# Row maxima of a two-pass attention softmax: high terms only, four heads at once in row strips, read from the transposed q and k

## The chip, the cores and the metric

The kernel runs on one core of a Trainium2 chip. The metric is the device time of one execution in microseconds (us). The engines are PE (TensorE, matmuls), DVE (VectorE), ACT (ScalarE), POOL (GpSimd) and SP (SyncE, which issues all DMAs here). Each has its own program, and semaphores order them.

## The reference, cut to what matters

Sixteen sequences of 256 tokens and 512 features pass through an adaptive RMS norm, 16-head self attention (32 features per head), an output projection with a skip, and a feed-forward with ternary weights and a GELU.

```python
q = _rms_norm(q, g_q); k = _rms_norm(k, g_k)
logits = jnp.einsum('bhqd,bhkd->bhqk', q, k) * d ** (-0.5)
attn = jax.nn.softmax(logits, axis=-1)
o = jnp.einsum('bhqk,bhkd->bhqd', attn, v)
o = o + o @ W_out
h = bitlinear(layer_norm(o), w_fc)       # 512 -> 2048, ternary weights
h = gelu(h)
x = x + bitlinear(layer_norm(h), w_proj) # 2048 -> 512, ternary weights
```

## The kernel before

Sequences are pipelined. One iteration works on five of them in different stages: `late` (end of the second feed-forward layer), `ffn` (output projection, first layer), `att` (attention), `qkv` (projections, transposes) and `pre` (statistics of the input). Iterations -2 to 17 run; the stages att and ffn are both present in 1 to 15. Iteration 0 has att without ffn and turns the feed-forward weights into ternary ones. Iteration 15 has no qkv stage, 16 no att.

Precision comes from splitting numbers into a high and a low half in f16. After the q and k projections, PE transposes four pieces into `T`, ACT writes the high part and DVE the low part of `qkT` (128 partitions = four heads of 32 features, by 4 groups, by LO_Q, HI_Q, HI_K, LO_K, by 256 tokens). SP then copies it with 16 DMAs into `stk`: for each of the 16 heads 96 rows that hold high and low parts stacked, so that one matmul with K=96 gives the full product. A 97th row holds minus the row maximum on one side and ones on the other.

Attention first computes for each head the logits with the queries on the partitions (L642, K=96, two matmuls of 256 columns, one for each half of the queries) in bank SA or SB, and DVE takes the maximum over the keys (L1039), one column of `rowmax`. When all 16 are there, PE transposes `rowmax` (L763), DVE negates it into `mrow` (L1128), and SP writes it as row 97 of the stack (L443). Then come the heads: the logits again, now with keys on the partitions and the maximum already subtracted by the 97th row (`scores`, L657), ACT's exponentials (L899, L905), DVE's low part (L1145) and the product with the values.

The order of PE in an iteration with all stages: output projection, the last quarter of the second layer of `late` with the transposes ("turn", L628) of the normalised ffn input and the first row maxima between them (PARTS, L45); eight units of the first layer (L753, L754: 16 matmuls each), row maxima between them (MAX_AFTER_UNIT, L47); after unit 6 the transpose of the maxima (MAX_TURN_UNIT); then the first piece of q and k, and the 16 heads with fillers between them. Unit n from 2 on waits for the GELU of unit n-2.

DVE goes through its own list in the same order: the low parts of the transposed input (yT_lo, L1111), the row maxima, `result` of late (L1066, which frees the bank of unit 1), and for each unit its row maxima and then the low part of the GELU output (L1132, called the hi/lo step here), which waits for ACT. After unit 2's step it has a tiny step msx (L1136). ACT does GELU, high part and square of each unit (L873, L878, L882). POOL adds up the GELU outputs and their squares, two sums (L535) for each unit from 1 on, 14 in all. Before, maximum k goes to bank k mod 2 and waits for maximum k-2 to be reduced.

Of the kernel before, what the change touches and what calls it, by code (L numbers as in the profile page):

```python
# [10 lines left out]
ALU = mybir.AluOpType  # L11
AX = mybir.AxisListType.X

P = 128
B, N, D = 16, 256, 512
HEADS = 16
DH = D // HEADS
F = 4 * D
TT = N // P
KT = D // P  # L20
FT = F // P
HPG = P // DH
GROUPS = HEADS // HPG
# [5 lines left out]
MROW = 3 * DH  # L29
STACK_ROWS = MROW + 1  # L30
ROW_COPIES = 4

LO_Q, HI_Q, HI_K, LO_K = range(4)
# [8 lines left out]

PARTS = [(), (), (4, 5, "turn", "max", 6), ("turn", 7, "max")]  # L45
MAX_AFTER_PART = [(), (), (0,), (1, 2)]
MAX_AFTER_UNIT = [(3, 4, 5), (6, 7), (8, 9), (10, 11), (12, 13), (14, 15), (), ()]  # L47
MSX_UNIT, MAX_TURN_UNIT = 2, 6
BEHIND = 2

# [36 lines left out]
def nth(b, per, k):  # L87

    return b * per + k
# [69 lines left out]
def adaln_ffn_kernel(nc, x, xT, condT, w_emb, b_emb, g_norm, g_qk, w_qkv, w_out, w_fcT, w_projT, out):  # L159
    with ExitStack() as ctx:  # L160
# [3 lines left out]
        def bank(name):  # L164
            return ctx.enter_context(nc.psum_tensor(name, [P, 512], F32))
# [48 lines left out]
        qkT = sb("qkT", [P, GROUPS, 4, N], F16)  # L214
# [53 lines left out]
        QB = [bank("QA"), bank("QB")]  # L268
# [2 lines left out]
        YT = [T, FB[1]]  # L271
        SB = [bank("SA"), bank("SB")]
        PV = bank("PV")


        ld_const = sem("ld_const")
# [278 lines left out]
        def _(pe):  # L555
# [35 lines left out]
            def iteration(i):  # L591
# [36 lines left out]
                        mm = pe.transpose(YT[t][:, k * P:(k + 1) * P], xn1[:, t, k * P:(k + 1) * P], ident[:, :])  # L628
                    mm.then_inc(turned, 1)

                def row_max(k):
                    if k % GROUPS == 0:
                        pe.wait_ge(dma_stk[k // GROUPS], nth(att, 16 * ROW_COPIES, 16 * ROW_COPIES))
                    if k < 2:
                        if live(att - 1):
                            pe.wait_ge(phi_r, nth(att - 1, HEADS, HEADS - 1 + k))
                        else:
                            pe.wait_ge(qkn_r, 3 + k)
                    else:
                        pe.wait_ge(max_r, nth(att, HEADS, k - 1))  # L640
                    for t in range(TT):
                        mm = pe.matmul(SB[k % 2][:, t * N:(t + 1) * N], stk[0:MROW, k, 0, t * P:(t + 1) * P],  # L642
                                       stk[0:MROW, k, 1, :], start=True, stop=True)
                    mm.then_inc(max_done, 1)

                def scores(h):

                    if h == 0:
                        pe.wait_ge(dma_m, nth(att, 16, 16))
                        if isinstance(att, int) and att == 0:  # L650
                            pe.wait_ge(s_ones, 1)
                    if h < 2:
                        pe.wait_ge(max_r, nth(att, HEADS, HEADS - 1 + h))
                    else:
                        pe.wait_ge(phi_r, nth(att, HEADS, h - 1))
                    for t in range(TT):
                        mm = pe.matmul(SB[h % 2][:, t * N:(t + 1) * N], stk[0:STACK_ROWS, place(h), 1, t * P:(t + 1) * P],  # L657
                                       stk[0:STACK_ROWS, place(h), 0, :], start=True, stop=True)
                    mm.then_inc(s_done, 1)
# [25 lines left out]
                def between(item):  # L685
                    kind, n, c = item
                    if kind == "qkv" and qkv is not None:
                        t, w = PIECES[n]
                        if n == 0 and c == 0:
                            pe.wait_ge(xlo_r, nth(qkv, KT, KT))  # L690
                            if isinstance(qkv, int) and qkv == 0:
                                pe.wait_ge(wq_l, KT)
                        if c == 0:
                            if first(qkv):
                                pass
                            elif n >= 2:
                                pe.wait_ge(qkn_r, nth(qkv, 4, n - 1))
                            elif ffn is not None:
                                pe.wait_ge(xn1_r, nth(ffn, TT, n + 1))
                            elif live(qkv - 1):  # L700
                                pe.wait_ge(vlo_r, nth(qkv - 1, TT, n + 1))
                        mm = qkv_mm(piece_bank(qkv, n)[:, :], t, w, c)
                        if c == KT - 1:
                            mm.then_inc(qk_done, 1)
                    if kind == "proj" and ffn is not None:
                        if isinstance(ffn, int) and ffn == 0:
                            if n == 1:
                                pe.wait_ge(s_tern, 8)
                            else:
                                pe.wait_ge(s_cs, 2)  # L710
                        second(ffn, n, c)
                    if kind == "v" and qkv is not None:
                        value_proj(n, c)
# [18 lines left out]
                for c in range(4):  # L732
                    for item in PARTS[c]:
                        if item == "turn" and ffn is not None:
                            y_turn(c - 2)
                        if item == "max" and att is not None:
                            for k in MAX_AFTER_PART[c]:
                                row_max(k)
                        if isinstance(item, int) and late is not None:
                            second(late, 0, item)  # L740
                for n in range(UNITS):
                    if ffn is not None:
# [10 lines left out]
                                pe.matmul(dst, w, yT_hi[:, k, :], start=(k == 0), stop=False)  # L753
                                mm = pe.matmul(dst, w, yT_lo[:, k, :], start=False, stop=(k == KT - 1))  # L754
                        mm.then_inc(fc_done, 1)
                    if att is not None:
                        for k in MAX_AFTER_UNIT[n]:
                            row_max(k)
                    if n == MAX_TURN_UNIT and att is not None:
                        pe.wait_ge(max_r, nth(att, HEADS, HEADS))  # L760
                        open_turn(("max", 0))
# [189 lines left out]
        def _(dve):  # L951
# [83 lines left out]
                                         v_hi[:, t, :, 0:DH], ALU.mult, ALU.subtract).then_inc(vlo_r, 1)  # L1035

            def row_max(att, k):
                dve.wait_ge(max_done, nth(att, HEADS, k + 1))
                dve.tensor_reduce(rowmax[:, :, k:k + 1].rearrange("p t o -> p (t o)"),  # L1039
                                  SB[k % 2][:, :].rearrange("p (t n) -> p t n", t=TT), AX, ALU.max  # L1040
                                  ).then_inc(max_r, 1)

            def heads_out(att, g):
# [32 lines left out]
            def iteration(i):  # L1076
# [30 lines left out]
                for c in range(4):  # L1107
                    if ffn is not None and c >= 2:
                        half_y = slice((c - 2) * P, (c - 1) * P)
                        dve.wait_ge(yhi_r, nth(ffn, TT, c - 1))  # L1110
                        dve.tensor_tensor(yT_lo[:, :, half_y], YT[c - 2][:, :].rearrange("p (k n) -> p k n", k=KT),  # L1111
                                          yT_hi[:, :, half_y], ALU.subtract).then_inc(unturned, 1)
                    if att is not None:
                        for k in MAX_AFTER_PART[c]:
                            row_max(att, k)
                if late is not None:
                    result(late, 0)
                for n in range(UNITS):
                    if isinstance(i, int) and i == 0 and n in FC_AT:
                        ternary(0, FC_AT[n])  # L1120
                    if att is not None:
                        for k in MAX_AFTER_UNIT[n]:
                            row_max(att, k)
                    if n == MAX_TURN_UNIT and att is not None:
                        dve.wait_ge(turned, turn(i, ("max", 0)) + 1)
# [138 lines left out]
```

## Time and profile before

| | |
|---|---|
| median of 3 runs | 1297.2 us (1296.57 to 1297.21) |
| span of the profiled execution | 1290.3 us |
| PE busy (matmul) | 1153.3 us, 89% |
| DVE busy | 990.3 us, 77% |
| ACT busy | 779.1 us, 60% |
| POOL busy | 607.4 us, 47% |
| chain that ended last | PE 57%, DVE 16%, issue 10%, ACT 5% |
| one steady iteration | 73.07 us |

The span goes from the first to the last instruction of one execution; the time of a run lies a few us above it. A share of busy time is an average over stages with different limits. The chain is followed back from the last instruction to whatever released each one; in it "issue" is time in which the engine waited for nothing that the profile shows. Matmuls overlap, so the duration of one (0.38 us for 256 columns) is longer than the distance to the next.

### The profile page before, as it was taken

The page shows a single profiled execution, that of the slowest core. Times are in us where ns is not written, and L with a number is a line of the kernel's source. Part 1 is how long each engine was busy: PE and PEld are TensorE (multiplying, and loading weights), DVE is VectorE, ACT ScalarE, POOL GpSimd, SP SyncE. Part 2 cuts the span into 40 slices and gives each one's busy share as a digit, 9 for nine tenths or more (in the row PEclk, how much of TensorE's full clock was granted, in tenths as well). Part 3 has the DMA queues.
Part 4 walks back from the last instruction along what each step waited for, and adds up shares of the span by engine and source line. Part 5 has one row for each costly group of instructions (what it writes and reads, how often), then busy time and mean ns, then how long its engine had stood idle before and what let it go on. Part 6 is the DMA issues. An engine that isn't in the chain of part 4 may idle for free.

```text
span 1290.3 us, 26563 instructions
## 1 busy us (share of the span) xinstructions
PE 1153.3 (89%) x9524; PEld 810.1 (63%) x9524; DVE 990.3 (77%) x1689; ACT 779.1 (60%) x1365; POOL 607.4 (47%) x369
## 2 busy tenths in 40 slices
PE   4746699999999999999999999999999999999796
PEld 4514466676666666676666666666667666676463
DVE  3496877887878787887878787887878787887743
ACT  3525366666657566675757576665757566675652
POOL 0436573461718264371728264461728264371515
PEclk9858999999999999999999999999999999999899
DMA  8250300303030110303030110303030110202001
GB/s 310 94 189 12 82 18 4 80 35 83 34 82 33 38 44 33 81 33 81 33 81 33 33 48 33 81 33 81 33 81 33 35 46 33 50 34 50 34 1 49
DMA packets 74445, 74.20 MB, mean 58 GB/s; under 512 B 6560, under 2 KB 55968, under 8 KB 73888
## 3 DMA queue, kind: packets, MB, share of 16 engines
q1 hardware_dynamic: 74400, 73.59, 18.9%
q8 instruction: 29, 0.48, 0.2%
q14 instruction: 16, 0.13, 0.0%
HBM read 39.89 MB, written 8.39 MB: 37 GB/s over the span
## 4 chain that ended last, share of the span: by engine, by line
PE 57%; DVE 16%; issue 10%; ACT 5%; POOL 1%; DVEq 0%; ACTq 0%; POOLq 0%
DVE rowmax L1039 8%; PE F L612 6%; PE F L614 6%; PE QB L582 4%; PE QA L582 4%; PE QA L584 4%; PE QA L583 4%; PE QB L583 4%; PE QB L584 4%; DVE hs L1132 3%; PE F L753 3%; PE F L754 2%; PE T L783 2%; PE SA L657 2%; PE SB L657 2%
## 5 line engine op out<-in xcount | busy, mean ns | idle before, releaser
L540 POOL TENSOR_TENSOR rqk<-msq,half 128x16 f32<-128x16 f32 x64 | 192.9, 3019 | 184.5 <-DVE msq L1165 183.8
L1145 DVE TENSOR_TENSOR p_lo<-p,p_hi 128x512 f16<-128x512 f32 x256 | 191.3, 749 | 77.2 <-ACT p_hi L905 70.9
L753 PE MATMUL F<-yT_hi,fc_t 128*128 128x256 f16 x1024 | 232.0, 274 | 3.5 <-DVE yT_lo L1111 3.4
L754 PE MATMUL F<-yT_lo,fc_t 128*128 128x256 f16 x1024 | 231.5, 273 | 0.0
L612 PE MATMUL F<-proj_t,hs 128*128 128x512 f16 x512 | 196.8, 384 | 5.1 <-DVE hs L1132 5.1
L535 POOL TENSOR_TENSOR acc<-acc,hgq 128x512 f32<-128x512 f32 x128 | 197.5, 1573 | 0.0
L614 PE MATMUL F<-proj_t,hs 128*128 128x512 f16 x512 | 196.3, 383 | 0.0
L522 POOL TENSOR_TENSOR rs<-var,half 128x1 f32<-128x1 f32 x32 | 17.7, 553 | 282.0 <-DVE var L1099 282.0
L1132 DVE SCALAR_TENSOR_TENSOR hs<-hgq,g_inv,hs 128x512 f16<-128x512 f32 x96 | 125.1, 1303 | 23.3 <-ACT hs L878 23.3
L672 PEld LDWEIGHTS PV<-v_hi,p_hi 128*128 128x128 f16 x1024 | 85.2, 96 | 59.9 <-issue 28.0
L535 POOL TENSOR_TENSOR acc<-hgq 128x512 f32<-128x512 f32 x32 | 47.2, 1479 | 152.5 <-ACT hgq L873 152.5
L899 ACT ACTIVATE p<-SA 128x512 f32<-128x512 f32 x128 | 76.8, 600 | 63.0 <-PE SA L657 61.3
L753 PEld LDWEIGHTS F<-yT_hi,fc_t 128*128 128x128 f16 x1024 | 100.3, 98 | 20.7 <-DVE yT_lo L1111 8.4
L672 PE MATMUL PV<-v_hi,p_hi 128*128 128x33 f16 x1024 | 105.9, 180 | 7.1 <-DVE o_sb L1051 3.6
L754 PEld LDWEIGHTS F<-yT_lo,fc_t 128*128 128x128 f16 x1024 | 100.6, 98 | 11.8
L674 PE MATMUL PV<-v_hi,p_lo 128*128 128x33 f16 x1024 | 103.6, 177 | 0.0
L673 PE MATMUL PV<-v_lo,p_hi 128*128 128x32 f16 x1024 | 103.5, 177 | 0.0
L899 ACT ACTIVATE p<-SB 128x512 f32<-128x512 f32 x128 | 76.5, 598 | 43.6 <-PE SB L657 42.0
L535 POOL TENSOR_TENSOR acc<-acc,sq 128x512 f32<-128x512 f32 x64 | 94.7, 1499 | 0.0
L1039 DVE TENSOR_REDUCE rowmax<-SB 128x2 f32<-128x512 f32 x128 | 87.2, 681 | 8.5 <-PE SB L642 8.3
L673 PEld LDWEIGHTS PV<-v_lo,p_hi 128*128 128x128 f16 x1024 | 84.0, 97 | 14.6 <-issue 0.6
L873 ACT ACTIVATE hgq<-F,g_fc 128x512 f32<-128x512 f32 x96 | 65.8, 685 | 43.3 <-PE F L754 40.9
(182 smaller groups left out, 2952.3 us busy)
## 6 DMA issues: line engine op xcount, KB each, us to landing
stk<-qkT SPq DMA_DIRECT2D x128, 128.0 KB, 2.5
xtok<-in_x SPq DMA_DIRECT2D x16, 512.0 KB, 3.5
xT_sb<-in_xT SPq DMA_DIRECT2D x16, 512.0 KB, 3.9
stk<-qkT SPq DMA_DIRECT2D x128, 64.0 KB, 2.1
xres<-in_x SPq DMA_DIRECT2D x16, 512.0 KB, 3.3
out<-xres SPq DMA_DIRECT2D x16, 512.0 KB, 2.8
stk<-in_w_emb SPq DMA_DIRECT2D x1, 2048.0 KB, 8.0
proj_t<-in_w_fcT SPq DMA_DIRECT2D x2, 1024.0 KB, 12.5
```

The lines of the kernel that those rows point to most:

```text
L535: pool.tensor_tensor(acc[:, s, :], a, src[n % 3][:, :], ALU.add).then_inc(sum_r, 1)
L540: pool.tensor_tensor(rqk[:, n % 2, :], msq[:, n % 2, :], half[:, :], ALU.pow).then_inc(rqk_r, 1)
L612: pe.matmul(FB[t][:, :], hs[:, 0, k // 2, col:col + P], proj_t[:, k, :], start=(k == 0), stop=False)
L614: mm = pe.matmul(FB[t][:, :], hs[:, 1, k // 2, col:col + P], proj_t[:, k, :], start=False, stop=(k == FT - 1))
L672: pe.matmul(dst, ph, v_hi[:, k, h, :], start=(k == 0), stop=False)
L673: pe.matmul(dst[:, 0:DH], ph, v_lo[:, k, h, :], start=False, stop=False)
L753: pe.matmul(dst, w, yT_hi[:, k, :], start=(k == 0), stop=False)
L754: mm = pe.matmul(dst, w, yT_lo[:, k, :], start=False, stop=(k == KT - 1))
L899: act.activation(p32[:, h % 2, :, :].rearrange("p k n -> p (k n)"), src, ACT.Exp, scale=LOGIT_SCALE).then_inc(p32_r, 1)
L1039: dve.tensor_reduce(rowmax[:, :, k:k + 1].rearrange("p t o -> p (t o)"), SB[k % 2][:, :].rearrange("p (t n) -> p t n", t=TT), AX, ALU.max) ...
L1132: dve.scalar_tensor_tensor(hs[:, 1, n, :], hg[n % 3][:, :], g_inv[:, 0:1], hs[:, 0, n, :], ALU.mult, ALU.subtract).then_inc(hlo_r, 1)
L1145: dve.tensor_tensor(p_lo[:, h % (BEHIND + 1), :, :], p32[:, h % 2, :, :], p_hi[:, h % (BEHIND + 1), :, :], ALU.subtract).then_inc(plo_r, 1)
```

## The change

The row maxima are computed from the high terms alone: K=32 instead of 96, with q and k read straight from `qkT`. Four heads of a group lie there in four strips of 32 partitions, and are multiplied in four row strips of the array into four banks (QA, QB, SA, SB). So there are four groups of eight matmuls instead of 16 pairs, group 0 behind the second turn and the end of the late second layer, groups 1, 2, 3 behind units 1, 3 and 5. A group waits until all four maxima of the group before are reduced. On DVE the reductions go in another order through the units: 0 and 1 ahead of the late result, then two ahead of each unit's hi/lo step up to unit 6. The wait for the stack's DMAs moves to the scores of heads 0 to 3. The column of `rowmax` changes with the order of the heads, so that `mrow` is the same as before. The scores themselves still use the stack.

```diff
-PARTS = [(), (), (4, 5, "turn", "max", 6), ("turn", 7, "max")]
-MAX_AFTER_PART = [(), (), (0,), (1, 2)]
-MAX_AFTER_UNIT = [(3, 4, 5), (6, 7), (8, 9), (10, 11), (12, 13), (14, 15), (), ()]
+PARTS = [(), (), (4, 5, "turn", 6), ("turn", 7, "max")]
+MAX_GROUP_AFTER_UNIT = {1: 1, 3: 2, 5: 3}
+FIRST_MAX = (0, 1)
+MAX_BEFORE_LOW = [(2, 3), (4, 5), (6, 7), (8, 9), (10, 11), (12, 13), (14, 15), ()]
...
+        MB = [QB[0], QB[1], SB[0], SB[1]]
...
-                def row_max(k):
-                    if k % GROUPS == 0:
-                        pe.wait_ge(dma_stk[k // GROUPS], nth(att, 16 * ROW_COPIES, 16 * ROW_COPIES))
-                    if k < 2:
+                def group_max(g):
+                    if g == 0:
+                        pe.wait_ge(qkhi_r, nth(att, 4, 4))
                         if live(att - 1):
-                            pe.wait_ge(phi_r, nth(att - 1, HEADS, HEADS - 1 + k))
+                            pe.wait_ge(phi_r, nth(att - 1, HEADS, HEADS))
                         else:
-                            pe.wait_ge(qkn_r, 3 + k)
+                            pe.wait_ge(qkn_r, 4)
+                        if ffn is not None:
+                            pe.wait_ge(xn1_r, nth(ffn, TT, TT))
+                        else:
+                            pe.wait_ge(vlo_r, nth(att, TT, TT))
                     else:
-                        pe.wait_ge(max_r, nth(att, HEADS, k - 1))
+                        pe.wait_ge(max_r, nth(att, HEADS, HPG * g))
                     for t in range(TT):
-                        mm = pe.matmul(SB[k % 2][:, t * N:(t + 1) * N], stk[0:MROW, k, 0, t * P:(t + 1) * P],
-                                       stk[0:MROW, k, 1, :], start=True, stop=True)
+                        for j in range(HPG):
+                            rows = slice(DH * j, DH * j + DH)
+                            mm = pe.matmul(MB[j][:, t * N:(t + 1) * N], qkT[rows, g, HI_Q, t * P:(t + 1) * P],
+                                           qkT[rows, g, HI_K, :], start=True, stop=True)
                     mm.then_inc(max_done, 1)
 
                 def scores(h):
 
+                    if h < GROUPS:
+                        pe.wait_ge(dma_stk[h], nth(att, 16 * ROW_COPIES, 16 * ROW_COPIES))
...
                     if h < 2:
-                        pe.wait_ge(max_r, nth(att, HEADS, HEADS - 1 + h))
+                        pe.wait_ge(max_r, nth(att, HEADS, HEADS))
...
+                            elif att is not None:
+                                pe.wait_ge(max_r, nth(att, HEADS, HEADS))
                             elif ffn is not None:
                                 pe.wait_ge(xn1_r, nth(ffn, TT, n + 1))
...
-                    if att is not None:
-                        for k in MAX_AFTER_UNIT[n]:
-                            row_max(k)
+                    if att is not None and n in MAX_GROUP_AFTER_UNIT:
+                        group_max(MAX_GROUP_AFTER_UNIT[n])
...
             def row_max(att, k):
-                dve.wait_ge(max_done, nth(att, HEADS, k + 1))
-                dve.tensor_reduce(rowmax[:, :, k:k + 1].rearrange("p t o -> p (t o)"),
-                                  SB[k % 2][:, :].rearrange("p (t n) -> p t n", t=TT), AX, ALU.max
+                g, j = k // HPG, k % HPG
+                if j == 0:
+                    dve.wait_ge(max_done, nth(att, GROUPS, g + 1))
+                col = j * GROUPS + g
+                dve.tensor_reduce(rowmax[:, :, col:col + 1].rearrange("p t o -> p (t o)"),
+                                  MB[j][:, :].rearrange("p (t n) -> p t n", t=TT), AX, ALU.max
                                   ).then_inc(max_r, 1)
...
-                    if att is not None:
-                        for k in MAX_AFTER_PART[c]:
-                            row_max(att, k)
+                if att is not None:
+                    for k in FIRST_MAX:
+                        row_max(att, k)
...
                     if att is not None:
-                        for k in MAX_AFTER_UNIT[n]:
+                        for k in MAX_BEFORE_LOW[n]:
                             row_max(att, k)
```

## Rows read from the trace of the kernel before

**Rows 1.** The page: span, then each engine's busy us, share and instruction count.

```profile
span 1290.3 us, 26563 instructions
...
PE 1153.3 (89%) x9524; PEld 810.1 (63%) x9524; DVE 990.3 (77%) x1689; ACT 779.1 (60%) x1365; POOL 607.4 (47%) x369
```

**Rows 2.** Stretches: length; busy us (count) of PE, PEld, DVE, ACT, POOL; clock; DMA; GB/s.

```profile
591.91:664.98 73.07, 69.23 (x593) 48.80 (x591) 58.97 (x103) 47.26 (x84) 35.43 (x22) 1.00 0.18 50
602.60:623.90 21.30, 18.30 (x157) 14.94 (x158) 20.03 (x25) 15.33 (x24) 15.18 (x11) 1.00 0.01 5
```

**Rows 3.** Timeline: start us, us, engine, line, output<-input, count, [idle before it <-releaser].

```profile
476.74 0.39 PE L763 MATMUL T<-ident,rowmax 128*16 128x128 f32 x2 [0.76 <-DVE rowmax L1039]
...
548.67 0.39 PE L763 MATMUL T<-ident,rowmax 128*16 128x128 f32 x2 [0.43 <-DVE rowmax L1039]
...
621.73 0.39 PE L763 MATMUL T<-ident,rowmax 128*16 128x128 f32 x2 [0.76 <-DVE rowmax L1039]
```

**Rows 4.** Timeline of PE around the first row maxima and unit 0.

```profile
599.31 0.38 PE L642 MATMUL SA<-stk 96*128 96x256 f16 x2
599.53 0.38 PE L612 MATMUL F<-proj_t,hs 128*128 128x512 f16 x1
...
602.62 0.28 PE L753 MATMUL F<-yT_hi,fc_t 128*128 128x256 f16 x1 [0.21 <-DVE yT_lo L1111]
```

**Rows 5.** Timeline of ACT: table load and the GELU of unit 1.

```profile
604.72 1.28 ACT L873 ACT_TABLE_LOAD   x1 [1.48 <-PE F L754]
...
607.97 0.67 ACT L873 ACTIVATE hgq<-F,g_fc 128x512 f32<-128x512 f32 x1
```

**Rows 6.** Timeline of POOL: the first two of the 14 sums.

```profile
608.71 1.27 POOL L535 TENSOR_TENSOR acc<-hgq 128x512 f32<-128x512 f32 x1 [9.56 <-ACT hgq L873]
...
609.99 1.68 POOL L535 TENSOR_TENSOR acc<-hgq 128x512 f32<-128x512 f32 x1
```

**Rows 7.** Timeline of DVE in the units.

```profile
607.57 0.75 DVE L1132 SCALAR_TENSOR_TENSOR hs<-hgq,g_inv,hs 128x512 f16<-128x512 f32 x1 [0.88 <-ACT hs L878]
...
609.44 1.09 DVE L1132 SCALAR_TENSOR_TENSOR hs<-hgq,g_inv,hs 128x512 f16<-128x512 f32 x1
...
611.65 1.79 DVE L1132 SCALAR_TENSOR_TENSOR hs<-sq,g_inv,hs 128x512 f16<-128x512 f32 x1
613.37 1.23 DVE L1136 TENSOR_SCALAR msx<-ssx 128x2 f32<-128x2 f32 x1
...
618.69 1.78 DVE L1132 SCALAR_TENSOR_TENSOR hs<-hgq,g_inv,hs 128x512 f16<-128x512 f32 x1
620.39 0.68 DVE L1039 TENSOR_REDUCE rowmax<-SA 128x2 f32<-128x512 f32 x1
...
621.59 1.78 DVE L1132 SCALAR_TENSOR_TENSOR hs<-sq,g_inv,hs 128x512 f16<-128x512 f32 x1
623.29 0.40 DVE L1128 TENSOR_SCALAR mrow<-T 16x256 f16<-16x256 f32 x1
```

**Rows 8.** Timeline of DVE in a shorter iteration.

```profile
543.78 0.73 DVE L1132 SCALAR_TENSOR_TENSOR hs<-hgq,g_inv,hs 128x512 f16<-128x512 f32 x1
```

**Rows 9.** Two stretches, and two neighbouring matmuls of PE's timeline.

```profile
94.00:96.00 2.00, 2.00 (x6) 1.54 (x5) 1.64 (x2) 1.57 (x1) 0.00 (x0) 0.50 1.04 394
614.00:616.00 2.00, 0.80 (x7) 0.26 (x5) 2.00 (x4) 1.83 (x4) 2.00 (x3) 1.00 0.00 0
...
93.04 0.63 PE L584 MATMUL QA<-wq_hi,xn_lo 128*128 128x512 f32 x1
93.46 0.63 PE L582 MATMUL QA<-wq_hi,xn_hi 128*128 128x512 f32 x1
```

**Rows 10.** Iteration 0: the first scores on PE.

```profile
98.97 0.39 PE L657 MATMUL SA<-stk 97*128 97x256 f16 x2 [1.56 <-DMA stk<-mrow]
```

**Rows 11.** Timeline of PE, iteration 15.

```profile
1204.57 0.39 PE L657 MATMUL SA<-stk 97*128 97x256 f16 x2 [1.75 <-DMA stk<-mrow]
...
1207.27 0.61 PE L657 MATMUL SA<-stk 97*128 97x256 f16 x2 [2.09 <-ACT p_hi L905]
```

More of the change, by code:

```diff
@@ L736, in iteration @@
                         if item == "max" and att is not None:
-                            for k in MAX_AFTER_PART[c]:
-                                row_max(k)
+                            group_max(0)
                         if isinstance(item, int) and late is not None:
@@ L755, in iteration @@
                         mm.then_inc(fc_done, 1)
-                    if att is not None:
-                        for k in MAX_AFTER_UNIT[n]:
-                            row_max(k)
+                    if att is not None and n in MAX_GROUP_AFTER_UNIT:
+                        group_max(MAX_GROUP_AFTER_UNIT[n])
                     if n == MAX_TURN_UNIT and att is not None:
@@ L1112, in iteration @@
                                           yT_hi[:, :, half_y], ALU.subtract).then_inc(unturned, 1)
-                    if att is not None:
-                        for k in MAX_AFTER_PART[c]:
-                            row_max(att, k)
+                if att is not None:
+                    for k in FIRST_MAX:
+                        row_max(att, k)
                 if late is not None:
```

## The prediction

> **What bounds the kernel now.** I read the page first: PE is busy 89% of the span, DVE 77% [rows 1]. That looks like a kernel that pays for every matmul, but it is an average. So next a table by stretch. A steady iteration lasts 73.07 us, and 21.3 us of it are the eight first-layer units; there DVE is busy 20.0 us and PE 18.3 us [rows 2]. Then the timeline, for which of them the other waits. PE transposes the row maxima (L763) after unit 6 and stands idle before it, released by the last reduction, at 621.73 [rows 3]. Everything behind it on PE (unit 7, the first query/key piece, 16 heads) follows in program order.
>
> Does a delay of that one transpose reach the end? Four of the 15 iterations with both stages answer. In them one hi/lo step (L1132, unit 3) took 0.73 us instead of 1.86 us [rows 8], and the transpose came 71.93 us after the one before; the next came 73.06 us later, as usual, so nothing caught up [rows 3]. 1.13 us on DVE ahead of the transpose is 1.13 us of period. The kernel is bound there by DVE's order, not by PE's work.
>
> DVE's order itself keeps step with POOL. The hi/lo step of unit 0, before POOL's sums start, takes 0.75 us; in unit 1 it takes 1.09, in unit 2 1.79; the tiny msx step takes 1.23 [rows 7]. POOL's sums take 1.27 us, but 1.68 where such a step comes between [rows 6]. From step 2 on, step starts lie 2.90 us apart (618.69, 621.59) [rows 7]. I read: a DVE step with its inputs in SBUF waits until POOL's running sum is over, holds POOL for some 0.45 us, and two reductions (1.20 us from the first's start to the next step's) [rows 7] bring DVE back to just behind POOL's next start. One unit of that is one interrupted and one plain sum, 1.68 + 1.27, less small overlaps: the 2.90 us. The Trainium skill (SBUF — State Buffer, "Who interferes with whom") says the same: a VectorE instruction with two SBUF inputs contends with GpSimd's reads by an exclusive lock, a reduction never. The trace agrees.
>
> **The change part by part.**
> (1) Row-max matmuls. Before: 32 per iteration at 0.11 us (a pair from 599.31 to the next at 599.53) [rows 4], 3.5 us of PE. After: 32 in groups of eight, four row strips and four banks. PE's own time lies wholly ahead of a transpose that waits for DVE, except group 0, which stands ahead of unit 0. Bounds for a group of eight: 0.22 us if four really run together, 0.88 us one after another at the spacing of today, 3.0 us if none is pipelined (8 x 0.38, the duration in [rows 4]). I take 0.88, the nearest row: same column count, nearly the same form.
> The Trainium skill (TensorE: Matmul & The Clock Gate, "Part 3") gives 3.07x for four strips of K=32. By it a group is 0.3 us, and as an estimate the sum below would be smaller by 0.17 us per iteration (from the second yT_lo on, (2) is held by DVE), 2.5 us in all.
> (2) Start of unit 0. Today PE does max 0 at 599.31, then a part of the second layer and the turn of y, and unit 0 at 602.62, released by yT_lo [rows 4]. Without max 0 the turn is ready once xn1 is, about 0.2 us sooner, and DVE takes the second yT_lo straight after the first, no reduction between: 602.25 instead of 602.62. PE arrives at unit 0 at 600.22 + 0.44 + 0.87 (second layer) + 0.88 (group 0) = 602.4. Gain 0.2 us (0.37 if the group is short). ACT's table load and the GELU of unit 1 follow [rows 5], and POOL starts at 608.71 - 0.22 = 608.49 [rows 6].
> (3) DVE's order, the heart of it. Before, reductions stood 3 ahead of unit 0, then 3, 2, 2, 2, 2, 2, so that the 16th came ahead of the hi/lo step of unit 5. Now 2, then 2 per unit, and the last two stand behind the hi/lo step of unit 5. Follow it: reductions 0 and 1 at 602.7 to 603.9, the late result to 604.6, 2 and 3 to 605.8, then 1.5 us of waiting for ACT, step 0 at 607.35 to 608.0, 4 and 5 to 609.25. Step 1 finds POOL's first sum running, as it did before (609.44), and is let in at its end, 0.22 us sooner than before. From here steps and sums run in the same lock step as before, two reductions between two steps, msx behind step 2, so each step ends 0.22 us sooner than it did: step 5 at 623.37 - 0.22 = 623.15. Before, the transpose came 1.26 us behind the end of step 4 (618.69 + 1.78 = 620.47, two reductions, 621.73) [rows 3, 7]; now it comes 1.26 us behind the end of step 5, at 624.40. Later by 2.67 us: one unit of 2.90 less about 0.22.
> (4) PE waits. Group 1 needs reduction 3 (605.8) after unit 1 (606.4): free. Group 2 needs reduction 7: 0.7 us idle. Group 3 needs reduction 11 (618.5) while unit 5 is done near 615.85: 2.7 us idle, with unit 6 queued behind. Then 3.2 us ahead of the transpose, with unit 7, the first piece and all heads behind it. DVE doesn't starve by it: reductions 8 and 12 want their groups at 614.3 and 620.15, which are there at 612.6 and 619.8. That second slack is 0.35 us; a group of 3.0 us would use it up.
> (5) mrow. Today it waits behind the step of unit 5, until 623.29 [rows 7]; now DVE waits 0.5 us for the transposed maxima and writes it at 624.8. Its DMA then has until 629.3, when the first scores are due: hidden. The steps of units 6 and 7 and POOL's last two sums slip too, by less than PE does.
> (6) Reading qkT instead of the stack moves the wait for SP's 16 stack DMAs to the scores. It cost 1.3 us in the whole run at one place where DVE wasn't ready anyway; its cover now is the unit stage. Nothing. The extra wait of the first piece for the last maximum is met at the transpose.
> (7) The edges. Iteration 15 has no first piece, and its first scores already wait for mrow's DMA [rows 11]; mrow there, as elsewhere, is written when (5) says, 0.4 us behind the moved transpose and not, as now, 1.57 us behind the old one (623.29 - 621.73): 2.67 + 0.45 - 1.57 = +1.55. Iteration 0 has no units: each group is a round trip, reduction to PE to reduction, with nothing on DVE to hide it, at the lower clock of 1.2 GHz (granted 0.50) [rows 9]. Three round trips at 0.9 to 2.1 us, the first scores waiting for mrow's DMA [rows 10]: +2.4 to +6.6, I take +4.
>
> Sum: 14 x 2.67 = 37.4, plus 1.6, plus 4, is 43.0. Span 1290.3 + 43.0 = 1333.3. The runs' median is 1297.2, 6.9 above the span, so 1340.2. Fewer row-max matmuls in time, but a slower kernel.
>
> **Rivals.**
> (A) Faster: PE's work pays after all. If PE were what the transpose waits for, 32 x 0.11 would shrink to a quarter, 2.6 us in each of 15 iterations: 1297 - 39 = 1258. It decides if PE reaches the transpose later than reduction 15. The 0.43 to 0.76 us of idle before it [rows 3] speak against; PE's 89% speaks for. 7%.
> (B) Near no change: the delay is caught up behind. Then 1297 to 1303. It needs slack ahead of the next DVE-bound stage; the 71.93 us iteration speaks against. 4%.
> (C) The lock falls otherwise: DVE's step beats POOL's start once more per iteration, 1.13 us as in [rows 8]. Then 14 x (2.67 - 1.13) + 5.6 = 27.2, 1324. Step 3 did so in 4 of 15 iterations, steps 4 and 5 never. 12%.
> (D) The granted clock falls. Idle of 2.7 and 3.2 us with 2.6 us of work between is more than any steady iteration shows; 0.8 us busy in 2 us left the clock at 1.00, the higher level of 2.4 GHz [rows 9]. In iteration 15 it had fallen after waits of 1.75 and 2.09 us with 0.6 us of work between (the same matmul pair took 0.39, then 0.61) [rows 11]. At 0.50 a matmul of 512 columns is spaced 0.42 us instead of 0.23 [rows 9], so unit 7 and the first piece cost 16 x 0.11 + 12 x 0.19 = 4.0 us more: 1400 if in every iteration, 1360 in a third of them. 17%.
> (E) The strips aren't pipelined, or switching between strips and the full array costs: up to 2.0 us ahead of unit 0 and 1.7 at group 3, 1340 + 15 x 3.7 = 1395 at worst, 1355 for a group of 1.9 us. The trace shows no cost where 97-row and 128-row matmuls alternate. 5%.
> The Trainium skill (TensorEngine Tiling (Array Packing), "Key Properties") says that a change of tiling mode drains TensorE. It is the rule behind (E); the trace of before doesn't show it.
> That the strips run one after another and not side by side isn't a rival of its own: the sum above assumes it.
>
> **How the numbers follow.** The forecast, 1328 to 1350, holds 55%; (C) 12, (D) 17, (E) 5, (A) 7, (B) 4. The range 1315 to 1370 takes in the forecast, (C), the lighter half of (D) and most of (E), about 80%. A measurement can tell about 0.2%, 2.6 us, from no change. Faster: (A) and a little, 8%. Within 0.2%: (B), 4%. Slower: 88%.
>
> **What would show it.** Right: the transpose L763's counterpart comes 17.0 us behind the step of unit 0 instead of 14.2 (621.73 - 607.57); the period is near 75.7; PE is idle about 2.7 us before group 3 and 3 us before the transpose; the reductions' count and 0.60 us spacing are unchanged; step 5 stands before the last two. Wrong at (3) if reductions 14 and 15 end before 623; at (1) if unit 0 starts later than 602.6 in that frame; at (7) if iterations 0 and 15 make more than 8 us of the difference. A clock under 1.00 in a steady stretch means (D); a transpose that waits for nothing means (A).

## The result, and the profile after

The changed kernel takes 1358.7 us (median of 4, 1347.1 to 1364.1) where the kernel before took 1296.9 us in the same comparison: a ratio of 1.047 (95% interval 1.042 to 1.052), 62 us slower. The forecast was 1340.2 us, the range 1315 to 1370. The sign, the mechanism and its size per steady iteration were as forecast. What stands on top is rival (D), the granted clock, which I had given 17%. It cost more than the 18 us between forecast and median, because two terms of the forecast were too high (see the sum further down).

The page of the changed kernel, span and busy times, answers to [rows 1]:

```profile
span 1353.5 us, 26597 instructions
...
PE 1151.0 (85%) x9524; PEld 791.1 (58%) x9524; DVE 976.5 (72%) x1689; ACT 773.4 (57%) x1365; POOL 594.1 (44%) x369
```

No engine is busy for longer than before, and yet the span is 63.2 us longer. So the engines wait more. PE also does part of its work at a lower clock; its sum doesn't show that, probably since the strips take less of its time. Now the timeline of PE at the transpose of the maxima (start, us, instruction, idle before it); the L772 here is the L763 of [rows 3]:

```profile
343.11 0.39 PE L772 MATMUL T<-ident,rowmax 128*16 128x128 f32 x2 [1.92 <-DVE rowmax L1051]
...
418.75 0.39 PE L772 MATMUL T<-ident,rowmax 128*16 128x128 f32 x2 [2.08 <-DVE rowmax L1051]
...
574.27 0.60 PE L772 MATMUL T<-ident,rowmax 128*16 128x128 f32 x2 [2.67 <-DVE rowmax L1051]
...
652.60 0.60 PE L772 MATMUL T<-ident,rowmax 128*16 128x128 f32 x2 [2.83 <-DVE rowmax L1051]
```

From 343.11 to 418.75 is 75.64 us; the forecast was 75.7, before it was 73.06. From 574.27 to 652.60 is 78.33 us, and there the pair of transposes takes 0.60 us and not 0.39: TensorE is at its lower clock. DVE's timeline of that iteration answers to [rows 7]:

```profile
635.59 0.75 DVE L1144 SCALAR_TENSOR_TENSOR hs<-hgq,g_inv,hs 128x512 f16<-128x512 f32 x1 [1.96 <-ACT hs L887]
...
649.58 1.77 DVE L1144 SCALAR_TENSOR_TENSOR hs<-sq,g_inv,hs 128x512 f16<-128x512 f32 x1
651.27 0.68 DVE L1051 TENSOR_REDUCE rowmax<-SA 128x2 f32<-128x512 f32 x1
651.87 0.68 DVE L1051 TENSOR_REDUCE rowmax<-SB 128x2 f32<-128x512 f32 x1
...
653.33 0.41 DVE L1140 TENSOR_SCALAR mrow<-T 16x256 f16<-16x256 f32 x1 [0.79 <-PE T L772]
```

The last two reductions stand behind unit 5's step, and the transpose starts 652.60 - 635.59 = 17.01 us behind unit 0's step; the forecast said 17.0. Next the clock, first over the whole iteration, then by stretches of 2 us (length, busy us and count of PE, PEld, DVE, ACT and POOL, granted clock, DMA share, GB/s):

```profile
574.27:652.60 78.33, 70.38 (x590) 48.07 (x591) 58.37 (x103) 46.77 (x84) 34.53 (x23) 0.94 0.16 47
644.00:646.00 2.00, 0.00 (x0) 0.00 (x0) 2.00 (x2) 1.86 (x4) 2.00 (x2) 1.00 0.00 0
...
648.00:650.00 2.00, 1.77 (x10) 0.95 (x8) 2.00 (x4) 0.12 (x1) 2.00 (x2) 0.55 0.00 0
650.00:652.00 2.00, 0.00 (x0) 0.00 (x0) 2.00 (x3) 1.81 (x3) 2.00 (x2) 0.50 0.00 0
652.00:654.00 2.00, 1.40 (x7) 1.02 (x8) 1.21 (x3) 0.00 (x0) 1.69 (x2) 0.50 0.00 0
...
658.00:660.00 2.00, 2.00 (x9) 1.48 (x8) 1.72 (x2) 0.77 (x2) 2.00 (x2) 0.89 0.00 0
```

PE stands still before group 3 (3.02 us) and again before the transpose (2.83 us), and the clock goes to 0.50 between the two. Unit 7 and the first half of the first piece, which wait behind the transpose, run at 1.2 GHz.

### The profile page after: what moved, and what is told of

It is laid out like the page before. It is cut to its first block, busy times and chain, and to the rows that moved or that the text cites. A ratio compares the mean times of both kernels' runs of the same rounds, so it can differ in the third digit from the quotient of the medians.

```text
span 1353.5 us, 26597 instructions
## 1 busy us (share of the span) xinstructions
PE 1151.0 (85%) x9524; PEld 791.1 (58%) x9524; DVE 976.5 (72%) x1689; ACT 773.4 (57%) x1365; POOL 594.1 (44%) x369
## 4 chain that ended last, share of the span: by engine, by line
PE 57%; DVE 18%; issue 7%; ACT 5%; SPq 1%; POOL 0%; DMA 0%; DVEq 0%; ACTq 0%; POOLq 0%
DVE rowmax L1051 8%; PE F L614 7%; PE F L616 7%; DVE hs L1144 7%; PE QA L584 4%; PE QB L584 4%; PE QA L585 4%; PE QA L586 4%; PE QB L586 4%; PE QB L585 4%; PE F L763 3%; PE F L764 3%; PE T L792 2%; PE SA L666 2%; PE SB L666 2%
## 5 line engine op out<-in xcount | busy, mean ns | idle before, releaser
L763 PE MATMUL F<-yT_hi,fc_t 128*128 128x256 f16 x1024 | 258.4, 294 | 5.0 <-DVE yT_lo L1123 4.5
L764 PE MATMUL F<-yT_lo,fc_t 128*128 128x256 f16 x1024 | 258.4, 294 | 0.0
L1157 DVE TENSOR_TENSOR p_lo<-p,p_hi 128x512 f16<-128x512 f32 x256 | 186.4, 728 | 91.2 <-ACT p_hi L914 82.0
L537 POOL TENSOR_TENSOR acc<-acc,hgq 128x512 f32<-128x512 f32 x128 | 182.5, 1445 | 42.1 <-ACT hgq L882 41.9
L1144 DVE SCALAR_TENSOR_TENSOR hs<-hgq,g_inv,hs 128x512 f16<-128x512 f32 x96 | 115.3, 1201 | 82.5 <-ACT hs L887 82.5
L763 PEld LDWEIGHTS F<-yT_hi,fc_t 128*128 128x128 f16 x1024 | 107.2, 105 | 44.0 <-DVE yT_lo L1123 9.4
L764 PEld LDWEIGHTS F<-yT_lo,fc_t 128*128 128x128 f16 x1024 | 107.6, 105 | 17.6
L584 PE MATMUL QA<-wq_hi,xn_hi 128*128 128x512 f32 x188 | 88.8, 472 | 4.1 <-DVE xn_lo L1038 4.1
```

The lines of the kernel that those rows point to most:

```text
L537: pool.tensor_tensor(acc[:, s, :], a, src[n % 3][:, :], ALU.add).then_inc(sum_r, 1)
L584: pe.matmul(dst, x_hi, w_hi, start=first, stop=False)
L1144: dve.scalar_tensor_tensor(hs[:, 1, n, :], hg[n % 3][:, :], g_inv[:, 0:1], hs[:, 0, n, :], ALU.mult, ALU.subtract).then_inc(hlo_r, 1)
L1157: dve.tensor_tensor(p_lo[:, h % (BEHIND + 1), :, :], p32[:, h % 2, :, :], p_hi[:, h % (BEHIND + 1), :, :], ALU.subtract).then_inc(plo_r, 1)
```

## Experiments

Every kernel is compared with the kernel before on the same chip; there that one took 1287 to 1292 us.

**Form and order apart.** The change has two halves. The first kernel takes only the form (K=32, read from `qkT`), still one head at a time in two banks; the second takes only the order.

```diff
-                        mm = pe.matmul(SB[k % 2][:, t * N:(t + 1) * N], stk[0:MROW, k, 0, t * P:(t + 1) * P],
-                                       stk[0:MROW, k, 1, :], start=True, stop=True)
+                        mm = pe.matmul(SB[k % 2][:, t * N:(t + 1) * N], qkT[rows, g, HI_Q, t * P:(t + 1) * P],
+                                       qkT[rows, g, HI_K, :], start=True, stop=True)
```

> Only the form changes: maxima from the high parts, K=32, read from the transposed q and k, but one head at a time in two banks at the old places, and DVE's old order. Order theory (the delay is two reductions behind unit 5's step): the transpose of the maxima stays 14.2 us behind unit 0's step, time within 0.3% of before, about 1297 us. Form theory (strips, the array's switching or the new operands cost time): a visible share of the 62 us, above 1305 us.

Measured: 1291.8 us beside 1287.2, ratio 1.0023 (1.0006 to 1.0040). In its trace the transpose stands 13.0 or 14.1 us behind unit 0's step, as before. If the form costs anything, it is 0.2%. Four strips side by side don't occur in this kernel; they are in the kernels further down.

```diff
-MAX_AFTER_PART = [(), (), (0,), (1, 2)]
-MAX_AFTER_UNIT = [(3, 4, 5), (6, 7), (8, 9), (10, 11), (12, 13), (14, 15), (), ()]
+MAX_AFTER_PART = [(), (), (), (0, 1)]
+MAX_AFTER_UNIT = [(2, 3), (4, 5), (6, 7), (8, 9), (10, 11), (12, 13), (14, 15), ()]
```

> Only the order changes: maxima stay K=96 from the stack in two banks, but stand two to a unit, ending behind unit 6 on PE and behind unit 5's step on DVE. Order theory: the transpose comes 17.0 us behind unit 0's step and the period grows by 2.7 to 2.9 us, so at least 1297 + 43 = 1340 us; where the granted clock falls in some iterations, up to 1360. Form theory: 1297 us, since nothing of the form changed.

Measured: 1334.0 and 1351.8 us beside 1287.2, and 1354.6 and 1354.7 in two further executions. That is 47 to 68 us more, as large as the changed kernel's 62. The old matmuls in the new order are enough for the slowdown. Timeline of DVE around its last reductions, then PE's transpose:

```profile
725.58 1.77 DVE L1132 SCALAR_TENSOR_TENSOR hs<-sq,g_inv,hs 128x512 f16<-128x512 f32 x1
727.28 0.68 DVE L1039 TENSOR_REDUCE rowmax<-SA 128x2 f32<-128x512 f32 x1
727.88 0.68 DVE L1039 TENSOR_REDUCE rowmax<-SB 128x2 f32<-128x512 f32 x1
...
728.61 0.39 PE L763 MATMUL T<-ident,rowmax 128*16 128x128 f32 x2 [2.50 <-DVE rowmax L1039]
```

That is 17.03 us behind unit 0's step, like the changed kernel. Half-clock matmuls appear here too, with K=96 and no strips, and PE is never idle for longer than 2.5 us in a steady iteration. So the falling clock isn't a matter of the strips.

**One edit of the order undone.** In the changed kernel only reductions 14 and 15 go back ahead of unit 5's step.

```diff
-MAX_BEFORE_LOW = [(2, 3), (4, 5), (6, 7), (8, 9), (10, 11), (12, 13), (14, 15), ()]
+MAX_BEFORE_LOW = [(2, 3), (4, 5), (6, 7), (8, 9), (10, 11), (12, 13, 14, 15), (), ()]
```

> The changed kernel with one edit in DVE's order: reductions 14 and 15 stand ahead of unit 5's step again, behind 12 and 13. Order theory: from unit 0's step to the transpose 15.3 us instead of 17.0 (end of step 4 at 12.9, four reductions 2.4, 0.1 on), so 1.7 us less per iteration, with a shorter wait before the transpose; 1300 us where the clock holds, up to 1325 where it still falls. Rival (the four-bank groups make the change slow, not their place beside step 5): no gain, 1345 to 1360 us.

Measured: 1298.9 us (1297.2 to 1304.2) beside 1291.3, ratio 1.006 (1.004 to 1.008). Two neighbouring transposes:

```profile
624.99 0.39 PE L772 MATMUL T<-ident,rowmax 128*16 128x128 f32 x2 [1.84 <-DVE rowmax L1051]
...
698.92 0.39 PE L772 MATMUL T<-ident,rowmax 128*16 128x128 f32 x2 [0.51 <-DVE rowmax L1051]
```

They stand 15.3 us behind unit 0's step, and the period is 73.93 us instead of 75.64. Two reductions of 0.6 us each, moved past one step, carry 1.7 us per iteration, an estimate of 26 us in 15 iterations. The clock still fell in unit 6 in seven iterations, but behind the transpose it was 1.00 in every one from the first on. Together that takes back 48 of the 55 us by which the changed kernel is slower on this chip (1346.6 us, below). Four strips and four banks are all still there, so they can account for no more than the 7.6 us that are left, the longer order included.

**The clock.** The changed kernel with work put into its two long waits: 16 matmuls (FILL) whose results nobody reads, ahead of group 3 and ahead of the transpose.

```diff
+                def fill():
...
+                        for c in range(FILL):
+                            pe.matmul(T[:, 0:N], fc_t[:, c % KT, 0:P], yT_hi[:, c % KT, :], start=True, stop=True)
...
+                    if n == 5 and att is not None:
+                        open_turn(("max", 0))
+                        fill()
                     if att is not None and n in MAX_GROUP_AFTER_UNIT:
...
+                        open_turn(("max", 0))
+                        fill()
                         pe.wait_ge(max_r, nth(att, HEADS, HEADS))
-                        open_turn(("max", 0))
```

> The changed kernel with 16 more matmuls of 256 columns (1.75 us, results not used) in each of PE's two long waits, before group 3 and before the transpose of the maxima. Clock theory (the 18 us beyond the forecast are the granted clock falling to 0.50 in those waits): the clock stays at 1.00 through all steady iterations, the period is 75.6 us without exception, about 1340 us although PE does more. Rival (the rest is something else, a cost of the strips or of the banks): 1359 us or more.

Measured: 1324.1 us (1322.1 to 1326.4) beside 1287.2, ratio 1.029 (1.026 to 1.032). PE has 32 more matmuls in each iteration, and the kernel is only 37 us slower than the one before, where the changed kernel is 55 to 62. The transposes, and the clock around one:

```profile
713.53 0.39 PE L782 MATMUL T<-ident,rowmax 128*16 128x128 f32 x2 [1.80 <-DVE rowmax L1061]
...
788.11 0.39 PE L782 MATMUL T<-ident,rowmax 128*16 128x128 f32 x2 [1.80 <-DVE rowmax L1061]
...
863.76 0.39 PE L782 MATMUL T<-ident,rowmax 128*16 128x128 f32 x2 [1.80 <-DVE rowmax L1061]
...
711.00:713.00 2.00, 0.73 (x7) 0.40 (x5) 2.00 (x3) 1.06 (x2) 2.00 (x2) 1.00 0.00 0
```

Every pair from iteration 1 on takes 0.39 us, and the granted clock is 1.00 in every steady iteration. The periods are 75.65 us, or 74.57 us where unit 3's step got through at once: the two values of before (73.06 and 71.93) plus 2.6 us. I expected 1340 and got 1324. The quick step came in 10 of 12 iterations (2 to 13) against 4 of 12 in the trace of before; at 1.1 us each that is 7 of the 16 us. The others are terms that the forecast itself had too high (see the sum further down).

Next, only the wait before the transpose is filled (the first `fill()` is left out), and the changed kernel is run beside it.

> The changed kernel with the 16 filler matmuls only in the wait before the transpose, not in the one before group 3. If the wait before the transpose alone lets the clock fall, 1324 us as with both filled and a clock of 1.00 in every steady iteration. If the wait before group 3 does it as well, some iterations still fall, 1330 to 1350 us.

> The changed kernel unedited, beside its edited forms on the same chip. Clock theory: 1345 to 1365 us, 20 to 35 us above the form with both waits filled (1324), and more spread between runs than any form in which the clock holds. Rival: it comes out at 1324 here, and the fillers did nothing.

Measured beside 1291.3: 1326.7 us (1323.3 to 1334.1) with one wait filled, 1346.6 us (1341.1 to 1361.1) unedited. With one wait filled, the clock still fell in unit 6 in 8 iterations, and it cost nearly nothing, since unit 6 ends in the wait: the transpose came late once, by 0.96 us. What costs time is a clock that is low behind the transpose, and there it was 1.00 in every iteration. So the fillers are worth 20 us beside the unedited kernel on the same chip, and the other 35 us are the order and the edges.

**POOL's lock.** The width of POOL's sums is cut to 16 of 512 columns; the sums, their waits and their count stay. The statistics of the second norm lack the other columns.

```diff
-                            pool.tensor_tensor(acc[:, s, :], a, src[n % 3][:, :], ALU.add).then_inc(sum_r, 1)
+                            pool.tensor_tensor(acc[:, s, 0:16], a[:, 0:16], src[n % 3][:, 0:16], ALU.add).then_inc(sum_r, 1)
```

> The kernel before with POOL's sums cut to 16 of 512 columns (the statistics of the second norm come out wrong; the sums' instructions, waits and count stay). Lock theory: DVE's hi/lo steps wait for POOL's running sum, so they fall from 1.78 to 0.75 us in every unit; DVE then waits for ACT, whose steps come about 2.1 us apart, and the transpose of the maxima comes about 10.2 us behind unit 0's step instead of 13.0 to 14.2: some 3 to 4 us less per iteration. Rival (the steps are slow for their own reasons, such as ACT or memory): steps stay near 1.8 us and the time near 1287.

> The changed kernel with the same cut sums (second norm wrong). Order theory: the transpose still stands one step and two reductions behind where it stood, now worth about 2.1 us (ACT's pace) instead of 2.9, so about 12.3 us behind unit 0's step, and it stays slower than the kernel before with cut sums by 2 us per iteration or more. Rival (the lock alone makes the change slow): both kernels with cut sums take the same time.

Measured: 1243.5 us with the order of before, 1250.7 us with the changed one (single executions; the kernel before took 1292.3). A step with reductions behind it and the transpose of each kernel, the old order first:

```profile
666.45 0.75 DVE L1132 SCALAR_TENSOR_TENSOR hs<-hgq,g_inv,hs 128x512 f16<-128x512 f32 x1
667.30 0.69 DVE L1039 TENSOR_REDUCE rowmax<-SA 128x2 f32<-128x512 f32 x1
...
671.25 0.38 PE L763 MATMUL T<-ident,rowmax 128*16 128x128 f32 x2
```

```profile
674.83 0.74 DVE L1144 SCALAR_TENSOR_TENSOR hs<-sq,g_inv,hs 128x512 f16<-128x512 f32 x1
675.49 0.68 DVE L1051 TENSOR_REDUCE rowmax<-SA 128x2 f32<-128x512 f32 x1
676.09 0.68 DVE L1051 TENSOR_REDUCE rowmax<-SB 128x2 f32<-128x512 f32 x1
...
676.82 0.39 PE L772 MATMUL T<-ident,rowmax 128*16 128x128 f32 x2 [1.45 <-DVE rowmax L1051]
```

Every step takes 0.75 us: the rest of the 1.8 us was the wait for POOL's sum. But my 2 us per iteration between the two orders were wrong. The periods are 69.79 and 70.10 us, 0.3 us apart. With free steps the old order's transpose has no idle before it; it waits for PE's own work (10.9 us behind unit 0's step, not 10.2). In the new order it comes 11.5 us behind that step, not 12.3: DVE works without a break there. A step and two reductions take it 1.9 us, and it doesn't wait for ACT as I had assumed. With these short sums the order costs 0.3 us per iteration and not 2.6. Each of the two has one trace.

**Unit 7 ahead of the transpose**, on PE alone, in both kernels.

```diff
+PE_TURN_UNIT = 7
...
-                    if n == MAX_TURN_UNIT and att is not None:
+                    if n == PE_TURN_UNIT and att is not None:
                         pe.wait_ge(max_r, nth(att, HEADS, HEADS))
```

> The kernel before with unit 7 ahead of the transpose of the maxima on PE, nothing else moved. PE's 0.76 us of idle before the transpose goes; mrow is written when it was, since it waits for unit 5's step. If the transpose's wait is the only limit, 14 x 0.76 to 0.83 = 11 us less, 1286 us. Rival: the mrow DMA (1.9 us behind mrow) or POOL takes its place, 1290 to 1297 us.

> The changed kernel with unit 7 ahead of the transpose on PE. The transpose stays 17.0 us (15.9 in the short iterations) behind unit 0's step, but 1.75 us of PE's work no longer stand behind it, and the wait before it shrinks from 3.5 to 1.8 us. Order and clock theory: 1324 us of the kernel with filled waits less 14 x 1.75 = 1300 us if the clock holds, up to 1315 if the wait of 2.7 us before group 3 still lets it fall. Rival (work behind the transpose is hidden anyway): 1355 us as the changed kernel.

Measured: 1282.6 us beside 1287.2 in the old kernel, ratio 0.9966 (0.9950 to 0.9982), a gain of 4.5 us and not 11. PE now has no idle before the transpose in any iteration: it is the one that comes late. Iterations with the quick step gain 0.1 us (period 71.80 against 71.93), the others 0.46 us; in those PE still waits for reductions ahead of its last row maxima (0.24 and 0.21 us). In the changed kernel: 1304.7 us (1298.6 to 1306.6) beside 1292.3, ratio 1.010 (1.009 to 1.012), as expected. Unit 7 takes 1.75 us and stands in front of the late release now; beside the kernel with filled waits that is 25 us less (12 us above before instead of 37), and 14 x 1.75 is 24.5.

**A version from the findings.** The new form in pairs of strips, so that a pair waits only for the pair two before; eight reductions ahead of unit 0's step, the last two ahead of unit 4's; mrow ahead of unit 5's step, and PE's transpose behind unit 7.

```diff
+MAX_PAIRS_AFTER_UNIT = {0: (2,), 1: (3, 4), 2: (5,), 3: (6,), 4: (7,)}
 FIRST_MAX = (0, 1)
-MAX_BEFORE_LOW = [(2, 3), (4, 5), (6, 7), (8, 9), (10, 11), (12, 13), (14, 15), ()]
+MAX_BEFORE_LOW = [(2, 3, 4, 5, 6, 7), (8, 9), (10, 11), (12, 13), (14, 15), (), (), ()]
-MSX_UNIT, MAX_TURN_UNIT = 2, 6
+MSX_UNIT, MAX_TURN_UNIT, PE_TURN_UNIT = 2, 5, 7
```

> A version made from the findings: the new form, but the four banks used as two pairs, each pair of strips waiting only for the pair two before; eight reductions ahead of unit 0's step, two each ahead of the steps of units 1 to 4, mrow written ahead of unit 5's step, unit 7 ahead of the transpose on PE. Order theory: the last reduction ends one unit earlier than before, 11.2 us behind unit 0's step; unit 7 is done by then, and the first scores come 3 us sooner. POOL's sums end where they did, so its first rqk can gain only 1.4 us: 1.4 to 3.4 us per iteration, 1240 to 1266 us beside 1287 of before. Rival (DVE's total work in the stage is the limit, whatever its order): 1280 to 1287 us.

Measured: 1282.8 us beside 1292.3, ratio 0.991 (0.989 to 0.994). The last reduction came where I wanted it (the transpose 10.8 or 11.9 us behind unit 0's step), and the first scores came 3.0 us sooner (15.9 us behind that step, where the kernel before has them at 18.9). But the time moved by 1% only, 17 us above the end of what I had expected. The wait had moved. POOL's and DVE's timelines behind the units:

```profile
627.53 6.26 POOL L542 TENSOR_TENSOR rqk<-msq,half 128x16 f32<-128x16 f32 x2 [1.43 <-DVE msq L1182]
```

```profile
623.20 1.77 DVE L1090 SCALAR_TENSOR_TENSOR xres<-res,c,xres 128x512 f32<-128x512 f32 x1
624.90 1.75 DVE L1162 TENSOR_TENSOR p_lo<-p,p_hi 128x512 f16<-128x512 f32 x1
626.57 0.67 DVE L1179 TENSOR_REDUCE ssq<-sq 128x16 f32<-128x512 f32 x1
```

The heads now begin while POOL still adds, so DVE's next two steps with inputs in SBUF take 1.8 us each, and the sum of squares that POOL waits for stands behind them. The last kernel moves it ahead of the first head's low part, and the late residual behind the second head's.

```diff
-                if late is not None:
-                    residual(late, 0)
                 for h in range(HEADS):
+                    if qkv is not None and h == 0 and h in square_at(qkv):
+                        square_sum(qkv, 0)
...
+                    if h == 1 and late is not None:
+                        residual(late, 0)
```

> The version with pairs of strips, with two steps of DVE moved: the sum of squares of the first piece goes ahead of the first head's low part, and the late residual behind the second head's. In the version with pairs POOL had ended its sums 1.4 us before its first rqk could start, which waited for DVE behind two lock waits of 1.8 us. Lock theory: rqk starts up to 1.4 us earlier, 1262 to 1278 us. Rival (the low parts of the heads, now later, hold the values on PE): 1278 to 1290 us, no gain.

```profile
623.98 6.65 POOL L542 TENSOR_TENSOR rqk<-msq,half 128x16 f32<-128x16 f32 x2
```

Measured: 1274.1 us (1273.1 to 1276.6) beside 1291.3, ratio 0.986 (0.983 to 0.988). POOL goes from its sums to rqk without idle. This version beats both kernels with the same K=32 matmuls as the changed one, in pairs and at other places.

## Why the prediction was right, and where it was off

**(1), (2) Form.** The place of this term was right, its size wrong. The four strips do run side by side: in the changed kernel a group's matmuls start in fours. The rows begin with the last matmul of unit 1 and end with the first of unit 2.

```profile
400.27 0.27 PE L764 MATMUL F<-yT_lo,fc_t 128*128 128x256 f16 x1
400.48 0.28 PE L649 MATMUL QA<-qkT 32*128 32x256 f16 x1
400.48 0.28 PE L649 MATMUL QB<-qkT 32*128 32x256 f16 x1
400.48 0.28 PE L649 MATMUL SA<-qkT 32*128 32x256 f16 x1
400.49 0.28 PE L649 MATMUL SB<-qkT 32*128 32x256 f16 x1
400.60 0.27 PE L649 MATMUL QA<-qkT 32*128 32x256 f16 x1
400.60 0.27 PE L649 MATMUL QB<-qkT 32*128 32x256 f16 x1
400.60 0.27 PE L649 MATMUL SA<-qkT 32*128 32x256 f16 x1
400.61 0.27 PE L649 MATMUL SB<-qkT 32*128 32x256 f16 x1
400.91 0.28 PE L763 MATMUL F<-yT_hi,fc_t 128*128 128x256 f16 x1
```

Four strips start within 0.01 us, the next four 0.12 us later: the eight matmuls take about 0.24 us and not 0.88. The Trainium skill (TensorE: Matmul & The Clock Gate, "Part 3") gives 3.07x for four strips of K=32 (measured there with 512 columns), an estimate of 0.3 us for a group; the trace agrees for the matmuls alone. But from the last matmul of unit 1 to the first of unit 2 it is 0.64 us, where two neighbours of a unit stand 0.11 apart. So a group takes 0.53 us of PE, and 0.3 of them lie at the two changes between the full array and the strips. The kernel with the form alone shows such a cost too: four matmuls of K=32 in one strip between two units make that distance 0.74 us, four of K=96 before made it 0.55. PE thus was given some 1.4 us per iteration (32 x 0.11 less 4 x 0.53), not the 2.6 of rival (A), and none of it reached the end. The upper bound of 3.0 us was misread as well: 0.38 us in [rows 4] is a pair of matmuls, one of 256 columns takes 0.27. Unit 0's step stood 58.9 us behind the transpose of the iteration before and now, where the clock held, stands 58.6 behind it, 0.3 us sooner; I had said 0.2, or 0.37 for a short group.

**(3) DVE's order.** Right. 17.0 us forecast from unit 0's step to the transpose, 17.01 to 17.04 measured; period 75.7 forecast, 75.64 measured where the clock held. That the order does it is shown by the kernel with the order alone and by the one that undoes it. Over the 11 periods of iterations 3 to 13, 2.58 us make 28.4 us. The periods of iterations 2 and 14 grew by less, 1.3 and 1.2 us, read from the kernel with filled waits (76.88 and 72.90 us against 75.56 and 71.70). I had priced them like the others.

**(4), rival (D) The clock.** The waits were forecast at 2.7 and 3.2 us and their effect left to a rival. Measured were 3.0 us before group 3 (1.9 with the quick step) and 1.9 to 3.5 us before the transpose. In the 11 periods of iterations 3 to 13 the changed kernel took 851.3 us where the undisturbed 75.66 (nine times) and 74.56 (twice) make 830.1: 21.3 us, 1.9 per iteration. Nine of the 11 periods were lengthened, more than the third of them that I had thought of. My price of 4.0 us for an iteration at half clock was too high. The dearest cost 2.8 (78.46 - 75.64), since the clock comes back during the first piece: the first scores stand 4.8 us behind the transpose at full clock and at most 7.6 us. That the clock is the cause is shown by the filled kernel. The step that failed is the choice of "no fall" as the likeliest case.

**(5), (6)** Right: mrow 0.5 us behind the transpose where the clock held and 0.7 where not (0.4 forecast), first scores not waiting for its DMA in a steady iteration, no wait for the stack's DMAs.

**(7) The edges.** Iteration 0: +4 forecast, its transpose came at 96.43 instead of 91.79, +4.6. Iteration 15: +1.55 forecast. Its transpose came 1.26 us later behind that of iteration 14 (72.45 against 71.19), and what follows it became 1.1 us shorter, so +0.1 in all. The shortening is what (7) forecast for mrow: it is written 0.42 us behind the transpose instead of 1.56, and the first scores stand 2.93 us behind it instead of 3.88.

**Sum.** The spans differ by 63.3 us (1353.54 - 1290.27): 4.6, then 0.4 up to the next transpose, 58.1 for the 13 periods of iterations 2 to 14, 1.3, and -1.1. Of the 58.1 us the clock took 25.8: the 21.3 of (4), and 4.5 in the periods of iterations 2 and 14 (78.71 and 75.62 us, where the filled kernel has 76.88 and 72.90). The order took 28.4 + 1.3 + 1.2 = 30.9, and one quick step fewer than before in iterations 3 to 13 took 1.1; 0.3 stay without a place.

So the order was forecast at 37.4 us in 14 iterations and measured at 31.3 (with the 0.4). The base was too high too: I put 6.9 us between span and time, but every later execution shows 1.8 (1353.5 and 1355.3 for the changed kernel). By that the profiled execution of before took some 1292.1 us, 5.1 less than the median that I started from. These two errors, 11 us together, hid almost half of the clock's 25.8. Without them the forecast would have been 1329 us and the miss 30 us and not 18: that it came so close is in part luck.

The quick step is a race that DVE wins or loses, worth 1.1 us each time: 4 wins in iterations 2 to 13 of the one traced execution of before, 8 with the form alone, 10 in the filled kernel. It is a likely part of the spread of the kernel before (1285 to 1297 us); no run shows how much of it.

**Rivals.** (A) and (B) fell: 1.7 us at the transpose are 1.7 us of period. (C) is real but not a matter of the change: the quick step came 4 times in 13 iterations (1 to 13) before and after. (E) has a true core, the 0.3 us at each group's two changes, but it is spent ahead of a transpose that waits for DVE. The order alone is as slow without strips, and with strips and two reductions moved back the kernel is within 0.6% of the one before.

## What to carry to other kernels

An engine at 89% can be the one that waits. Look for the release that most work is queued behind, and count what stands ahead of it on the releasing engine: the new order cost 2.6 us per iteration here, and putting two reductions of 0.6 us back ahead of one step returned 1.7 of them. The reductions themselves were no fewer. A wait has a second price if TensorE's clock falls in it and is still low behind the release; work put into the wait made this kernel 20 us faster. And after each gain look for the next lock or queue before sizing it.

## What the runs showed of the hardware

- Four matmuls of K=32 in four row strips start within 0.01 us (changed kernel); in one strip they stand 0.11 us apart and take 0.27 us each, as with K=96 (form alone). A set of them between matmuls of the full array took 0.2 us (one strip) to 0.3 us (four strips) of PE on top of their own spacing.
- In the changed kernel PE waits 3.0 us (or 1.9) before group 3 and 1.9 to 3.5 us before the transpose, and in nine of 11 periods part of the work behind the transpose ran at a granted clock of 0.50. With waits of 1.3 and 2.5 us (order alone) that happened too, behind 10 of the 12 transposes of iterations 2 to 13. With at most 1.3 and 1.8 us (waits filled) the clock stayed at 1.00 in every steady iteration.
- A DVE step with two inputs in SBUF took 0.75 us beside POOL sums of 16 columns. Beside sums of 512 columns steps 2, 4 and 5 took 1.77 to 1.79 us in every steady iteration before and after the change, and step 3, which follows msx, took 1.86 or 0.73 us.
